# Rotary attention of one layer: the mix written to four column quadrants, the output product on the diagonal of the array, the normalisation on ScalarE, the output product ahead of the scores

## The chip, the cores and the metric

One core of a Trainium2 chip runs the whole program. The metric is the time of one execution on the device, in microseconds (us). Before the change the median of three runs is 3659.68 us.

## What is computed

The program is a twelve-stage model over x (128 sequences of 32 rows, 128 wide). The change touches the second stage only:

```python
x = x + _L0_attn_ref(_layernorm(x, axis=-1), L0_attn_Wq, L0_attn_Wk, L0_attn_Wv, L0_attn_Wo)

def _L0_attn_ref(x, Wq, Wk, Wv, Wo):      # HQ 16, HKV 4, HD 8, WINDOW 32
    xq, xk = _rope(x @ Wq), _rope(x @ Wk); xv = x @ Wv
    keys = jnp.repeat(xk, N_REP, axis=2)
    values = jnp.repeat(xv, N_REP, axis=2)
    scores = jnp.einsum('bqhd,bkhd->bhqk', xq, keys) / math.sqrt(HD)
    scores = jnp.where(mask[None, None], scores, -jnp.inf)
    attn = jax.nn.softmax(scores, axis=-1)
    ctx = jnp.einsum('bhqk,bkhd->bqhd', attn, values).reshape(b, s, HQ * HD)
    return ctx @ Wo
```

## The kernel before

`rotary_attention` (L573) works on 32 tiles; a tile is 4 sequences of 32 rows, so 128 partitions by 128 columns of x. Each engine runs one function `step(t, j, live)`, in which it handles several tiles that are at different ages: `live(lag)` says that tile t - lag exists. `pipelined` unrolls the first steps and the last eight, and puts those between into a hardware loop of four steps per turn. There are 32 tiles and four buffers (W = 4) of everything; `bank_a` and `bank_b` are the two PSUM banks of a buffer. Each engine does its instructions strictly as written, and waits on semaphores. So the written order inside `step` is what sets the order of the work:

- TensorE (L763): transpose of the normalised tile t (L166, after the addition to x of tile t - 4, whose bank it takes); transposes of the probabilities of t - 3 (`turn`, L746); projection of t to q and k (L729) and to v (L732); mix of t - 3 (L754); scores of t - 1 (L739); output product of t - 3 (L761).
- ScalarE (L655): copy of the transposed tile t (L173), of the transposed probabilities of t - 3 (L640), of v of tile t (L648), exponential of t - 2 (L644), copy of the mix of t - 3 (L652).
- VectorE (L698): addition to x of t - 4 (L186), rotary terms of t - 1 (L686, L690), band, maximum and subtraction of t - 2 (L677, L711, L713), moments of x of tile t + 2 (L119, L122), sum and reciprocal of t - 2 (L694, L696), normalisation of t + 1 (L160).
- GpSimd (L625): division of the probabilities of t - 3 (L622), inverse deviation of t + 1 (L135, L142), the two masked operands of t - 1 (L616, L618).

The mix of a tile is four matmuls, one for each sequence b. Each gives 32 rows (head group and head width) by 128 columns (head and query), and all four write partitions 0 to 31 of the bank, one beside the other. The copy reorders 32 x 512 values to `mixT`, and four matmuls, one for each head h of a group, accumulate the 128 rows of output from 32 rows each.

## Time and profile before

| | |
|---|---|
| median of 3 runs | 3659.68 us (3658.84 to 3660.41) |
| profiled execution, its own time | 3661.03 us |
| its span, first to last instruction | 3659.1 us |
| mean granted TensorE clock | 0.932 of 2.4 GHz |
| TensorE busy in the span | 3278.6 us (90%) |
| the stage of the change, first load to last addition | 91.6 to 306.0 us |

The profile gives for each engine when an instruction started, how long it took, and what ended the idle time before it. PE is TensorE's matmuls, PEld its weight loads (they overlap), DVE is VectorE, ACT ScalarE, POOL GpSimd, SP the queue that issues transfers. A matmul in 32-bit floats leaves two records, a transpose one. The stage is 6% of the program, and stages follow each other, so what the stage gains or loses the program does.

### The profile page before, as it was taken

Reading aid. Unit: us, or ns where it says so; the run is one execution under the profiler, and the core shown is the slowest. Engines: PE = TensorE matmul, PEld = TensorE weight load, DVE = VectorE, ACT = ScalarE, POOL = GpSimd, SP = SyncE. Lnnn points to the kernel's source line nnn. Section 1 sums busy time; section 2 is a strip of 40 time slices with the busy share of each in tenths; the row PEclk is TensorE's granted clock in tenths of the full one; section 3 lists DMA queues with packets and bytes.
Section 4 is the critical chain, followed back from the end, with each engine's and each line's share of the span. In section 5 each row is a group of like instructions: output and inputs, shape, how many; then the busy total and the mean of one; then the engine's idle time right before and its main releaser. Section 6 shows DMA issues by size and latency. Waiting matters only on the chain. (4 is left out here: it accounts for less than half of the span.)

```text
span 3659.1 us, 108450 instructions
## 1 busy us (share of the span) xinstructions
PE 3278.6 (90%) x40814; PEld 2737.0 (75%) x40816; DVE 2575.0 (70%) x7254; ACT 1817.8 (50%) x4530; POOL 1245.0 (34%) x1823
## 2 busy tenths in 40 slices
PE   6887899999989999897999999999999999874866
PEld 4776889898867777645789898899889899643345
DVE  6784999999968888757565655555655656468765
ACT  3331777777757777664433333333333333224463
POOL 3562888888843333312400000000000000155032
PEclk8997999999989999998799999999999999867687
DMA  4001000000012222200275555555555555254000
GB/s 117 5 0 38 1 0 0 0 0 0 0 48 78 79 78 77 72 1 7 60 139 132 131 132 132 122 139 127 133 131 127 132 130 131 69 108 74 0 3 26
DMA packets 375492, 254.10 MB, mean 69 GB/s; under 512 B 118676, under 2 KB 371560, under 8 KB 374536
## 3 DMA queue, kind: packets, MB, share of 16 engines
q1 hardware_dynamic: 370824, 245.44, 28.0%
q10 hardware_dynamic: 4352, 4.20, 0.5%
q8 instruction: 229, 3.75, 0.5%
q14 instruction: 87, 0.71, 0.1%
HBM read 233.53 MB, written 15.75 MB: 68 GB/s over the span
## 5 line engine op out<-in xcount | busy, mean ns | idle before, releaser
L1062 PE MATMUL psum<-L_ffn_share,L_ffn_prob 128*128 128x128 f32 x4096 | 491.1, 279 | 45.9 <-DVE L_ffn_prob L995 38.3
L1062 PEld LDWEIGHTS psum<-L_ffn_share,L_ffn_prob 128*128 128x128 f32 x4096 | 473.5, 193 | 59.5 <-DVE L_ffn_prob L995 46.2
L878 POOL TENSOR_TENSOR L_ffn_sums<-L_ffn_sims 128x1024 f32<-128x1024 f32 x256 | 485.3, 1912 | 85.8 <-DVE L_ffn_prob L995 85.8
L2463 PE MATMUL psum<-L_xattn_ctxT,L_xattn_q_ctx 128*128 128x257 f32 x2048 | 510.6, 390 | 0.0
L2494 PEld LDWEIGHTS psum<-L_xattn_probT,L_xattn_ctx 32*128 32x128 f32 x16384 | 469.1, 187 | 44.6 <-issue 42.0
L2494 PE MATMUL psum<-L_xattn_probT,L_xattn_ctx 32*128 32x128 f32 x16384 | 493.4, 273 | 2.1 <-DVE L_xattn_probT L2377 2.1
L2315 ACT ACTIVATE L_xattn_prob<-psum,L_xattn_nmax 128x258 f32<-128x258 f32 x512 | 239.2, 472 | 480.1 <-DVE L_xattn_nmax L2363 463.5
L2286 POOL TENSOR_TENSOR L_xattn_z_var<-L_xattn_z_mv,L_xattn_z_eps 128x1 f32<-128x1 f32 x32 | 6.1, 192 | 1248.6 <-DVE L_xattn_z_mv L2389 1219.3
L2463 PEld LDWEIGHTS psum<-L_xattn_ctxT,L_xattn_q_ctx 128*128 128x128 f32 x2048 | 368.5, 191 | 62.2 <-issue 5.9
L920 ACT ACTIVATE psum<-L_ffn_sums,L_ffn_bias 128x512 f32<-128x512 f32 x512 | 339.2, 686 | 89.1 <-DVE L_ffn_prob L995 85.1
L995 DVE SCALAR_TENSOR_TENSOR L_ffn_prob<-L_ffn_sums,L_ffn_best,psum 128x512 f32<-128x512 f32 x512 | 358.1, 741 | 6.9 <-ACT psum L920 3.8
L1352 ACT ACTIVATE L_xattn_prob<-psum,L_xattn_nmax 128x289 f32<-128x289 f32 x512 | 250.0, 501 | 109.0 <-DVE L_xattn_nmax L1383 109.0
L2368 DVE RECIPROCAL L_xattn_total<-L_xattn_total 128x2 f32<-128x2 f32 x256 | 41.4, 162 | 245.7 <-ACT L_xattn_prob L2315 235.3
L1383 DVE TENSOR_REDUCE L_xattn_nmax<-psum 128x1 f32<-128x289 f32 x512 | 199.1, 451 | 14.2 <-PE psum L1421 7.9
L2309 ACT ACTIVATE L_xattn_q_heads<-psum 128x256 f32<-128x256 f32 x128 | 49.2, 384 | 320.3 <-PE psum L2435 320.3
L2377 DVE STREAM_TRANSPOSE L_xattn_probT<-L_xattn_prob 128x512 f32<-128x512 f32 x256 | 182.2, 712 | 19.4
L2363 DVE TENSOR_REDUCE L_xattn_nmax<-psum 128x2 f32<-128x516 f32 x256 | 178.2, 696 | 19.1 <-issue 0.4
L2371 DVE TENSOR_SCALAR L_xattn_prob<-L_xattn_prob,L_xattn_total 128x256 f32<-128x256 f32 x512 | 158.4, 351 | 21.6 <-issue 2.1
L2353 DVE COPY L_xattn_q_ctx<-psum 128x512 f32<-128x512 f32 x256 | 159.8, 664 | 17.1 <-PE psum L2447 17.1
L1421 PE MATMUL psum<-L_xattn_k_all,L_xattn_q_bd 32*128 32x289 f32 x1024 | 153.0, 460 | 13.7 <-DMA L_xattn_k_all<-ctx_T_dram 4.0
L2447 PE MATMUL psum<-L_xattn_q_heads,L_xattn_wk_cross 64*128 64x128 f32 x2048 | 154.3, 291 | 7.7 <-issue 5.2
L1437 PEld LDWEIGHTS psum<-const,L_xattn_prob 128*128 128x128 f32 x1024 | 111.3, 142 | 51.1 <-issue 49.9
(459 smaller groups left out, 6651.0 us busy)
## 6 DMA issues: line engine op xcount, KB each, us to landing
L_xattn_ctx<-ctx_dram SPq DMA_DIRECT2D x512, 256.0 KB, 3.9
L_xattn_ctxT<-ctx_T_dram SPq DMA_DIRECT2D x128, 257.0 KB, 3.3
L_xattn_k_all<-ctx_T_dram SPq DMA_DIRECT2D x128, 128.5 KB, 2.1
L_xattn_v_all<-ctx_dram SPq DMA_DIRECT2D x128, 128.0 KB, 2.2
L_attn_qkv_scratch<-L_attn_qkv SPq DMA_DIRECT2D x24, 256.0 KB, 2.8
L_attn_rows<-L_attn_qkv_scratch SPq DMA_DIRECT2D x24, 256.0 KB, 5.3
start_raw<-ctx_dram ACTq DMA_DIRECT2D x16, 256.0 KB, 11.9
L_xattn_v_rows<-L_xattn_v SPq DMA_DIRECT2D x8, 256.0 KB, 2.3
```

The lines of the kernel that those rows point to most:

```text
L878: nc.gpsimd.tensor_tensor(sums[:, h % RING, :, :], sx, sy, ALU.add).then_inc(summed, 1)
L920: nc.scalar.activation(raw_prob(k), half(sums[:, h % RING, :, :].rearrange("p i j -> p (i j)"), k), ACT.Exp, bias=bias[:, s, h:h + 1]).the ...
L995: nc.vector.scalar_tensor_tensor(half(prob[:, h % RING, :], k), half(sums[:, h % RING, :, :].rearrange("p i j -> p (i j)"), k), best[:, s, ...
L1062: last = nc.tensor.matmul(pair(2 * s)[:, c * P:(c + 1) * P], prob[:, h % RING, c * P:(c + 1) * P], share[:, h % RING, :], start=(h == 0 an ...
L1352: ins = nc.scalar.activation(prob[:, b % 2, g, :], scores(g), ACT.Exp, bias=nmax[:, b % 2, g:g + 1], accum_out=total[:, b % 2, g:g + 1])
L1383: nc.vector.tensor_reduce(nmax[:, b % 2, g:g + 1], scores(g), X, ALU.max, negate=True).then_inc(maxed, 1)
L2315: ins = nc.scalar.activation(prob[:, s, g, :], scores(s)[:, g, :], ACT.Exp, bias=nmax[:, s, g:g + 1], accum_out=total[:, s, g:g + 1])
L2353: nc.vector.tensor_copy(q_ctx[:, t % 2, c, :, 4 * j:4 * j + 4, :], core.psum[:, 2:4, :].rearrange("p e (a w) -> p (e a) w", a=2)[:, :, c * ...
L2363: nc.vector.tensor_reduce(nmax[:, s, :], scores(s), X, ALU.max, negate=True).then_inc(maxed, 1)
L2377: nc.vector.transpose(probT[:, b % 2, :, 2 * s:2 * s + 2, :].rearrange("p k g n -> p g k n"), prob[:, s, :, 0:2 * P].rearrange("p g (k m) ...
L2463: last = nc.tensor.matmul(scores(s)[:, g, 0:CTX], q_ctx[:, p, c, b, h:h + 4, :].rearrange("p h n -> p (h n)"), ctxT[:, b, c, :], start=(c ...
L2494: last = nc.tensor.matmul(mix_bank(r)[:, c * P:(c + 1) * P], ctx[rows, b, k, c * P:(c + 1) * P], probT[rows, b % 2, k, :, :].rearrange("p ...
```

## The change

- `mix`: the matmul of sequence b writes partitions 32b to 32b + 31, columns 0 to 127, so the four use four different column groups of the array. `mix_copy` copies 128 x 128 values without reordering in place of 32 x 512.
- `out`: sixteen matmuls in place of four. The one of head h and sequence b has rows 32b to 32b + 31 of `mixT` and `w_o`, and writes the same partitions of the bank: the diagonal 32 x 32 tiles of the array, b innermost. `w_o` holds the same weights four times, loaded with four transfers in place of one.
- `out` of tile t - 3 stands ahead of `score` of tile t - 1 on TensorE.
- The addition to x is that of tile t - 3, in the same step, after the moments and ahead of the sums on VectorE (before: of tile t - 4, first thing of the next step).
- The normalisation of t + 1 goes from VectorE (L160) to ScalarE, as an activation between the copy of v and the exponential. GpSimd gets one more small instruction a tile for its bias.
- TensorE's steps are all unrolled, without the hardware loop.

```diff
--- before.py
+++ after.py
@@ -582,7 +582,7 @@
         w_qk = sb("w_qk", [D, 4, D])
 
         w_v = sb("w_v", [D, G, G * 8])
-        w_o = sb("w_o", [G * 8, G, D])
+        w_o = sb("w_o", [P, G, D])
         qk = sb("qk", [P, W, 2, P])
         prod = sb("prod", [P, W, 2, P])
         q4 = sb("q4", [P, W, BT, G, SEQ])
@@ -591,20 +591,21 @@
         prob = sb("prob", [P, W, HEADS, SEQ])
         top = sb("top", [P, W, HEADS])
         total = sb("total", [P, W, HEADS])
+        shifted_mean = sb("shifted_mean", [P, W])
         probT = sb("probT", [P, W, BT, P])
-        mixT = sb("mixT", [G * 8, W, G, P])
+        mixT = sb("mixT", [P, W, G, SEQ])
         bank_a = lambda s: core.psum[:, 2 * s, :]
         bank_b = lambda s: core.psum[:, 2 * s + 1, :]
         front = Front(core, st, name, W, bank_a)
         (w_in, zeroed, projected, v_done, roped, masked, scored, shifted, exped, summed, normal, turned, probT_done,
-         mixed, mixT_done, out_done, added) = (core.sem(f"{name}_{n}") for n in (
+         mixed, mixT_done, out_done, added, centred) = (core.sem(f"{name}_{n}") for n in (
              "w_in", "zeroed", "projected", "v_done", "roped", "masked", "scored", "shifted", "exped", "summed",
-             "normal", "turned", "probT_done", "mixed", "mixT_done", "out_done", "added"))
+             "normal", "turned", "probT_done", "mixed", "mixT_done", "out_done", "added", "centred"))
         block = st.enter_context(nc.Block())
 
         @block.sync
         def _(sp):
-            load(sp, [(w_qk[:, :, :], dram[f"{name}_Wqk"]), (w_o[:, :, :], dram[f"{name}_Wo"])], w_in)
+            load(sp, [(w_qk[:, :, :], dram[f"{name}_Wqk"]), *((w_o[32 * b:32 * b + 32, :, :], dram[f"{name}_Wo"]) for b in range(BT))], w_in)
             sp.wait_ge(zeroed, 1)
             load(sp, [(w_v[:, g, 8 * g:8 * g + 8], dram[f"{name}_Wv"][:, 8 * g:8 * g + 8]) for g in range(G)], w_in)
 
@@ -617,6 +618,12 @@
                 a, m = spread(qk[:, s, 1, :].rearrange("p (b w) -> p b w", b=BT), core.c("group"), SEQ)
                 nc.gpsimd.tensor_tensor(kbd[:, s, :, :, :], a, m, ALU.mult).then_inc(masked, 1)
 
+            def normal_factors(t, s):
+                front.pool_rstd(pool, t - s, only=s)
+                pool.drain()
+                nc.gpsimd.tensor_scalar(shifted_mean[:, s:s + 1], front.mv[:, s, 0:1], front.rstd[:, s, :], -1.0, ALU.mult,
+                                        ALU.mult).then_inc(centred, 1)
+
             def normalise(t, s):
                 pool.wait_ge(summed, t + 1)
                 nc.gpsimd.tensor_tensor(prob[:, s, :, :], prob[:, s, :, :], per_row(total[:, s, :]),
@@ -626,7 +633,7 @@
                 if live(3):
                     normalise(t - 3, (j - 3) % W)
                 if live(-1):
-                    front.pool_rstd(pool, t + 1 - (j + 1) % W, only=(j + 1) % W)
+                    normal_factors(t + 1, (j + 1) % W)
                 if live(1):
                     mask(t - 1, (j - 1) % W)
 
@@ -639,6 +646,11 @@
                 act.wait_ge(turned, t + 1)
                 nc.scalar.copy(probT[:, s, :, :], bank_a(s).rearrange("p (b w) -> p b w", b=BT)).then_inc(probT_done, 1)
 
+            def normalise(t, s):
+                act.wait_ge(centred, t + 1)
+                nc.scalar.activation(front.xn[:, s, :], core.x[:, ds(t, 1), :].rearrange("p a d -> p (a d)"), ACT.Identity,
+                                     bias=shifted_mean[:, s:s + 1], scale=front.rstd[:, s, :]).then_inc(front.normed, 1)
+
             def exp(t, s):
                 act.wait_ge(shifted, t + 1)
                 nc.scalar.activation(prob[:, s, :, :], prob[:, s, :, :], ACT.Exp).then_inc(exped, 1)
@@ -649,8 +661,7 @@
 
             def mix_copy(t, s):
                 act.wait_ge(mixed, t + 1)
-                nc.scalar.copy(mixT[:, s, :, :].rearrange("p h (b q) -> p b h q", b=BT),
-                               bank_b(s)[0:G * 8, :].rearrange("p (b h q) -> p b h q", b=BT, h=G)).then_inc(mixT_done, 1)
+                nc.scalar.copy(mixT[:, s, :, :], bank_b(s)[:, 0:P].rearrange("p (h q) -> p h q", h=G)).then_inc(mixT_done, 1)
 
             def step(t, j, live):
                 if live(0):
@@ -659,6 +670,8 @@
                     turn_copy(t - 3, (j - 3) % W)
                 if live(0):
                     v_copy(t, j)
+                if live(-1):
+                    normalise(t + 1, (j + 1) % W)
                 if live(2):
                     exp(t - 2, (j - 2) % W)
                 if live(3):
@@ -696,10 +709,7 @@
                 nc.vector.reciprocal(total[:, s, :], total[:, s, :]).then_inc(summed, 1)
 
             def step(t, j, live):
-                o, q = (j - 1) % W, (j - 2) % W
-                if live(4):
-                    dve.wait_ge(out_done, t - 3)
-                    add_to_x(core, t - 4, bank_a(j)[:, 0:D]).then_inc(added, 1)
+                o, q, m = (j - 1) % W, (j - 2) % W, (j - 3) % W
                 if live(1):
                     turn_pairs(t - 1, o)
                     dve.drain()
@@ -713,10 +723,11 @@
                     nc.vector.tensor_tensor(prob[:, q, :, :], raw, per_row(top[:, q, :]), ALU.subtract).then_inc(shifted, 1)
                 if live(-2):
                     front.dve_moments(dve, t + 2 - (j + 2) % W, only=(j + 2) % W)
+                if live(3):
+                    dve.wait_ge(out_done, t - 2)
+                    add_to_x(core, t - 3, bank_a(m)[:, 0:D]).then_inc(added, 1)
                 if live(2):
                     sums(t - 2, q)
-                if live(-1):
-                    front.dve_normalise(dve, t + 1 - (j + 1) % W, only=(j + 1) % W)
 
             front.dve_moments(dve, 0, only=0)
             pipelined(dve, W, -1, 4, step)
@@ -751,14 +762,17 @@
                 pe.wait_ge(v_done, t + 1)
                 pe.wait_ge(probT_done, t + 1)
                 for b in range(BT):
-                    last = nc.tensor.matmul(bank_b(s)[0:G * 8, b * P:(b + 1) * P], vbd[:, s, b, :], probT[:, s, b, :],
+                    last = nc.tensor.matmul(bank_b(s)[32 * b:32 * b + 32, 0:P], vbd[:, s, b, :], probT[:, s, b, :],
                                             start=True, stop=True)
                 last.then_inc(mixed, 1)
 
             def out(t, s):
                 pe.wait_ge(mixT_done, t + 1)
                 for h in range(G):
-                    last = nc.tensor.matmul(bank_a(s)[:, 0:D], mixT[:, s, h, :], w_o[:, h, :], start=(h == 0), stop=(h == G - 1))
+                    for b in range(BT):
+                        own = slice(32 * b, 32 * b + 32)
+                        last = nc.tensor.matmul(bank_a(s)[own, 0:D], mixT[own, s, h, :], w_o[own, h, :], start=(h == 0),
+                                                stop=(h == G - 1))
                 last.then_inc(out_done, 1)
 
             def step(t, j, live):
@@ -772,13 +786,14 @@
                     project(t, j)
                 if live(3):
                     mix(t - 3, (j - 3) % W)
+                if live(3):
+                    out(t - 3, (j - 3) % W)
                 if live(1):
                     score(t - 1, (j - 1) % W)
-                if live(3):
-                    out(t - 3, (j - 3) % W)
-
-            pe.wait_ge(w_in, 16 * (2 + G))
-            pipelined(pe, W, -1, 4, step)
+
+            pe.wait_ge(w_in, 16 * (1 + BT + G))
+            for t in range(TILES + 4):
+                step(t, t % W, lambda lag: 0 <= t - lag < TILES)
 
 
 def product_key_experts(core, name):
```

Below, rows of the order in which the engines are given their work, first VectorE, from the band addition of one step to the addition to x. Before:

```order
L677 TENSOR_TENSOR psum<-psum,const 128x512
L711 TENSOR_REDUCE L_attn_top<-psum 128x16
L713 TENSOR_TENSOR L_attn_prob<-psum,L_attn_top 128x512
L119 ISA
L119 BN_STATS L_attn_front_stats_sb<-x_sb 128x6
L122 BN_AGGR L_attn_front_mv_sb<-L_attn_front_stats_sb 128x2
L694 TENSOR_REDUCE L_attn_total<-L_attn_prob 128x16
L696 RECIPROCAL L_attn_total<-L_attn_total 128x16
L160 TENSOR_SCALAR L_attn_front_xn_sb<-x_sb,L_attn_front_mv_sb,L_attn_front_rstd_sb 128x128
L186 ISA
L186 TENSOR_TENSOR x_sb<-x_sb,psum 128x128
```

VectorE, the same stretch of the changed kernel (its line numbers differ: L690, L721, L723 are the band, maximum and subtraction, L707 and L709 the sum and the reciprocal, L699 the first rotary product):

```order
L690 TENSOR_TENSOR psum<-psum,const 128x512
L721 TENSOR_REDUCE L_attn_top<-psum 128x16
L723 TENSOR_TENSOR L_attn_prob<-psum,L_attn_top 128x512
L119 ISA
L119 BN_STATS L_attn_front_stats_sb<-x_sb 128x6
L122 BN_AGGR L_attn_front_mv_sb<-L_attn_front_stats_sb 128x2
L186 ISA
L186 TENSOR_TENSOR x_sb<-x_sb,psum 128x128
L707 TENSOR_REDUCE L_attn_total<-L_attn_prob 128x16
L709 RECIPROCAL L_attn_total<-L_attn_total 128x16
L699 TENSOR_TENSOR psum<-psum,const 128x2x128
```

The addition L186 has moved from behind the sum and the reciprocal to ahead of them, and L160 is gone. ScalarE, one step of before:

```order
L173 COPY L_attn_front_xnT_sb<-psum 128x128
L640 COPY L_attn_probT<-psum 128x512
L648 COPY L_attn_vbd<-psum 128x128
L644 ACTIVATE L_attn_prob<-L_attn_prob 128x512
L652 COPY L_attn_mixT<-psum 32x4x4x32
```

and of the change (L656 is the exponential, L664 the copy of the mix):

```order
L173 COPY L_attn_front_xnT_sb<-psum 128x128
L647 COPY L_attn_probT<-psum 128x512
L660 COPY L_attn_vbd<-psum 128x128
L650 REGISTER_ALU
L651 ISA
L651 ACTIVATE L_attn_front_xn_sb<-x_sb,L_attn_shifted_mean,L_attn_front_rstd_sb 128x128
L656 ACTIVATE L_attn_prob<-L_attn_prob 128x512
L664 COPY L_attn_mixT<-psum 128x128
```

The normalisation L651 stands between the copy of v and the exponential, and the copy of the mix is still behind the exponential. TensorE, one step of before:

```order
L166 MATMUL psum<-const,L_attn_front_xn_sb 128x128
L746 MATMUL psum<-const,L_attn_prob 128x128 x4
L729 MATMUL psum<-L_attn_front_xnT_sb,L_attn_w_qk 128x128 x4
L732 MATMUL psum<-L_attn_w_v,L_attn_front_xnT_sb 32x32 x16
L754 MATMUL psum<-L_attn_probT,L_attn_vbd 32x128 x4
L739 MATMUL psum<-L_attn_kbd,L_attn_q 128x128 x4
L761 MATMUL psum<-L_attn_w_o,L_attn_mixT 128x128 x4
```

and of the change (L757 turns the probabilities, L740 and L743 project, L765 mixes, L774 is the output product, L750 the scores):

```order
L166 MATMUL psum<-const,L_attn_front_xn_sb 128x128
L757 MATMUL psum<-const,L_attn_prob 128x128 x4
L740 MATMUL psum<-L_attn_front_xnT_sb,L_attn_w_qk 128x128 x4
L743 MATMUL psum<-L_attn_w_v,L_attn_front_xnT_sb 32x32 x16
L765 MATMUL psum<-L_attn_probT,L_attn_vbd 32x128 x4
L774 MATMUL psum<-L_attn_w_o,L_attn_mixT 32x128 x16
L750 MATMUL psum<-L_attn_kbd,L_attn_q 128x128 x4
```

The output product has gone ahead of the scores and is sixteen matmuls of 32 output rows.

## Rows read from the trace of the kernel before

**Rows 1.** By stretch: length, PE, PEld, DVE, ACT, POOL busy (records), clock, DMA share, GB/s:
```profile
150.00:200.00 50.00, 44.30 (x563) 36.76 (x560) 40.52 (x100) 18.69 (x42) 30.67 (x41) 1.00 0.00 0
```

**Rows 2.** Timeline of one step: start, us, engine, line, operation [idle before <-releaser]
```profile
217.25 0.63 ACT L644 ACTIVATE L_attn_prob<-L_attn_prob 128x512 f32<-128x512 f32 x1 [0.63 <-DVE L_attn_prob L713]
...
217.79 0.56 ACT L652 COPY L_attn_mixT<-psum 32x512 f32<-32x512 f32 x1
...
218.40 1.15 PE L761 MATMUL psum<-L_attn_w_o,L_attn_mixT 32*128 32x128 f32 x8
...
219.70 0.29 DVE L186 TENSOR_TENSOR x_sb<-x_sb,psum 128x128 f32 x1 [0.53 <-PE psum L761]
...
220.80 1.16 PE L729 MATMUL psum<-L_attn_front_xnT_sb,L_attn_w_qk 128*128 128x128 f32 x8
...
221.89 0.46 PE L732 MATMUL psum<-L_attn_w_v,L_attn_front_xnT_sb 128*32 128x32 f32 x32
...
222.16 1.04 PE L754 MATMUL psum<-L_attn_probT,L_attn_vbd 128*32 128x128 f32 x8
...
222.43 0.27 ACT L648 COPY L_attn_vbd<-psum 128x128 f32<-128x128 f32 x1 [0.92 <-PE psum L732]
222.60 0.69 DVE L713 TENSOR_TENSOR L_attn_prob<-psum,L_attn_top 128x512 f32<-128x512 f32 x1
223.33 0.63 ACT L644 ACTIVATE L_attn_prob<-L_attn_prob 128x512 f32<-128x512 f32 x1 [0.64 <-DVE L_attn_prob L713]
...
223.99 0.69 DVE L694 TENSOR_REDUCE L_attn_total<-L_attn_prob 128x16 f32<-128x512 f32 x1
...
224.75 0.25 DVE L696 RECIPROCAL L_attn_total<-L_attn_total 128x16 f32<-128x16 f32 x1
```

**Rows 3.** Timeline, an early step where TensorE waited for the divided probabilities:
```profile
108.48 0.25 DVE L696 RECIPROCAL L_attn_total<-L_attn_total 128x16 f32<-128x16 f32 x1
...
108.82 1.05 POOL L622 TENSOR_TENSOR L_attn_prob<-L_attn_prob,L_attn_total 128x512 f32<-128x512 f32 x1 [2.77 <-DVE L_attn_total L696]
...
109.92 0.42 PEld L746 LDWEIGHTS psum<-const,L_attn_prob 128*128 128x128 f32 x4 [0.82 <-POOL L_attn_prob L622]
...
110.31 0.97 PEld L729 LDWEIGHTS psum<-L_attn_front_xnT_sb,L_attn_w_qk 128*128 128x128 f32 x8
```

**Rows 4.** Timeline, ScalarE: normalising activations of another stage, a copy ahead of the exponential:
```profile
75.60 1.65 ACT L494 ACTIVATE L_xattn_front_xn_sb<-x_sb,L_xattn_shifted,L_xattn_front_rstd_sb 128x128 f32<-128x128 f32 x4 [2.37 <-POOL L_xattn_shifted L476]
...
106.89 0.27 ACT L648 COPY L_attn_vbd<-psum 128x128 f32<-128x128 f32 x1 [1.68 <-PE psum L732]
107.06 0.64 ACT L644 ACTIVATE L_attn_prob<-L_attn_prob 128x512 f32<-128x512 f32 x1
```

**Rows 5.** Timeline, TensorE in two later attention stages: quarter-array matmuls that rotate over groups:
```profile
1303.38 0.65 PE L1470 MATMUL psum<-L_xattn_probT,L_xattn_v_all 128*32 128x128 f32 x16
1303.84 0.40 PE L1473 MATMUL psum<-L_xattn_endT,L_xattn_v_end 128*32 128x128 f32 x8
...
2399.73 1.83 PE L2494 MATMUL psum<-L_xattn_probT,L_xattn_ctx 32*128 32x128 f32 x57
```

**Rows 6.** Timeline, start of the stage, and the bias instruction in the next stage:
```profile
92.47 1.84 SPq L180 DMA_DIRECT2D L_attn_w_v<-L_attn_Wv_dram  x4
...
95.69 0.48 PE L166 MATMUL psum<-const,L_attn_front_xn_sb 128*128 128x128 f32 x1 [5.12 <-DMA L_attn_w_v<-L_attn_Wv_dram]
...
357.51 0.27 POOL L855 TENSOR_SCALAR L_ffn_shifted_mean<-L_ffn_front_mv_sb,L_ffn_front_rstd_sb 128x1 f32<-128x1 f32 x1 [0.20 <-issue]
```

**Rows 7.** Timeline: additions to x on either side of a fall of the clock:
```profile
121.25 0.29 DVE L186 TENSOR_TENSOR x_sb<-x_sb,psum 128x128 f32 x1 [0.53 <-PE psum L761]
...
128.45 0.29 DVE L186 TENSOR_TENSOR x_sb<-x_sb,psum 128x128 f32 x1 [1.19 <-PE psum L761]
```

**Rows 8.** Busy time by stretch: around the second fall, and in a later attention stage:
```profile
242.00:248.00 6.00, 5.43 (x62) 4.80 (x61) 4.91 (x13) 1.58 (x5) 3.81 (x5) 0.72 0.00 0
...
3300.00:3340.00 40.00, 29.33 (x659) 25.35 (x659) 38.90 (x75) 20.16 (x45) 33.97 (x46) 1.00 0.79 110
```

## The prediction

> **What bounds the kernel now.** I read three views: the busy time by stretch, to see whether an engine is full in this stage; the timeline of one step, for what each engine waits on; and the timeline of the stage's start. In the first [rows 1] TensorE is busy 44.3 of 50 us, VectorE 40.5, ScalarE only 18.7. No engine is full, so a ring of waits must set the pace. The reader should look at the exponential in the second view [rows 2]: it starts at 217.25 and again at 223.33, so a step is 6.08 us. The ring is closed like this. The subtraction starts at 222.60 and the exponential 0.73 later. The copy of the mix stands behind it on ScalarE and starts 0.54 after it (217.25 to 217.79). The output product starts 0.61 later (218.40), the addition to x 1.30 after that (219.70), and the next subtraction on VectorE 2.90 after the addition (222.60). 0.73 + 0.54 + 0.61 + 1.30 + 2.90 = 6.08, the whole step. VectorE idles 0.53 us in it, right before the addition, for the output product. The sum and the reciprocal are not in this ring: VectorE does them while ScalarE and TensorE finish the mix and the output.
>
> **The mix in quadrants** takes TensorE work away. Now it is 8 records in 1.04 us on one column group [rows 2]; 8 records that rotate over four groups took 0.40 [rows 5]. That is 0.6 us of TensorE a step, but the mix is not in the ring (its copy waits for the exponential), so I count 0. Its copy shrinks from 32 x 512 (0.56) to 128 x 128, which is the size of the copy of v (0.27) [rows 2]: minus 0.29 in the ring.
>
> **The output product** becomes 32 records of a quarter tile with 128 columns each. No row shows the diagonal. The nearest rows are quarter-array matmuls with 128 columns that rotate over groups: 16 records from 1303.38 to 1303.84, 29 ns each, and 57 in 1.83 us, 32 ns each [rows 5]. 32 of them are 0.92 to 1.03, and the last one's own tail adds about 0.2 (0.65 against 0.46 in the first row). I take 1.15, as now, because the rows with 128 columns are nearer than any other. The bounds: 0.46, which the 32 records with 32 columns took [rows 2], and 4.2, if they ran one after another like the mix of before (1.04 for 8). The rows for four row groups have one bank for each group; here all four write one bank, though different partitions. The Trainium skill (TensorEngine Tiling (Array Packing), Restrictions and Gotchas) says that different row tiles cannot access the same PSUM bank at once. By it the sum would be that of the serial rival below; by the rotating rows it is the 1.15. No trace here has row groups that share a bank, so neither is shown.
>
> **The addition ahead of the sums** is the costly edit. The output product of t - 3 still waits for the copy of the mix, which waits behind the exponential of t - 2. VectorE, which reaches the addition right after the moments, must now wait through exponential, copy and product, and only then does it sum and invert. Both were off the ring and come onto it: 0.76 for the sum (223.99 to 224.75) and 0.17 until the next instruction starts (the reciprocal is 0.25 long; the copy of v, 0.27 long, frees its engine after 0.17 [rows 4]). Ring: 6.08 - 0.29 + 0.76 + 0.17 = 6.72. Taking 0.26 us of normalisation off VectorE is worth nothing, since it stood in the time in which VectorE would have waited.
>
> **The normalisation on ScalarE** closes a longer ring. It stands behind the copy of v of tile t, and the exponential behind it. From the start of one reciprocal: 0.34 until GpSimd divides, 1.10 until TensorE turns, 0.39 until it projects [rows 3]; 1.09 until v, 0.54 until v is copied [rows 2]; 0.17 until the next ScalarE instruction, 0.41 for the normalisation (four in 1.65) [rows 4]; 0.54 for the exponential until the copy of the mix, 0.27 + 0.05 until the output product, 1.15 + 0.15 until the addition [rows 2]; 0.21 until the sum (an addition of 0.29, freeing the engine early as above), 0.76 until the next reciprocal. The sum is **7.17 us**, longer than 6.72, so this ring sets the step: plus 1.09. The exponential will start some 0.5 us after its subtraction has ended instead of 0.04.
>
> **The rest.** Scores behind the output product: with four matmuls of the projection's size (1.09 [rows 2]) they end about 4.90 + 1.15 + 1.09 = 7.1 into the step. The band addition wants them in the next step behind its rotary terms, so after 7.17 + 0.17. The cover is over 0.2 us, so 0; were it gone, the wait would come onto VectorE's part of the ring. GpSimd's new instruction: 0.20 idle and 0.27 [rows 6]; the masked operands come up to 0.5 later and still ahead of the scores' turn behind the product, so 0. Unrolled TensorE steps: the unrolled first steps of before ran without a gap of their own [rows 3], so 0. The three extra transfers of `w_o` stand ahead of those of `w_v` on SP's queue, four of which took 1.84 us, and TensorE's first transpose waits for the last of them [rows 6]: 3 x 0.46 = +1.4, once.
>
> **The clock.** Between the additions at 121.25 and 128.45 [rows 7] the step took 7.20, 1.12 more than normal; a stretch around the second such step shows a granted clock of 0.72, part of it at 1.2 GHz, although TensorE was 90% busy [rows 8]. There are two in the full steps of before. The change spreads less TensorE work over a longer step, with a gap before the output product and one before the turn, so I expect more of them. A later attention stage held 2.4 GHz through at 29.3 of 40 us busy [rows 8], which bounds the price from below at 0. From above I take 20 falls at 1.12, +22. I take four, +4, nearer the lower end because that stage's row is the one with comparable gaps.
>
> **The sum.** 28 steps have all ages in flight: 28 x 1.09 = 30.5. Three more drain without a projection and follow the 6.72 ring: 3 x 0.64 = 1.9. Transfers 1.4, clock 4. Together +38. The profiled execution took 3661.03 us, so 3699; the median of the runs shown is 1.35 below it. Forecast against the median: **3698 us**, 1.0% slower. About 0.2%, 7 us, is what a measurement of this kernel can tell from no change.
>
> **Rivals.**
> - *The clock falls often.* Every second or third step has a stretch at 1.2 GHz. For: it fell even at 90% busy [rows 8]. Against: the later stage at 73%. +34 + 22 = 3715 to 3722.
> - *The diagonal runs serially* (shared bank, as above): product 3.5 to 4.2 instead of 1.15, plus 2.4 to 3.0 on 31 steps, about 3780.
> - *Only the VectorE ring binds*, because the normalisation finds ScalarE free earlier than I think: 6.72 a step, 31 x 0.64 = 20, plus 1.4 and a little clock: about 3682.
> - *The other side: faster.* If the output product were ready when VectorE reaches the addition, VectorE's own work would be the bound: 6.08 less the 0.53 of waiting and less the 0.26 of L160, 5.3 us. 28 x -0.78 = -22, so 3639. It decides only if the product no longer waits for an exponential on ScalarE. The order on ScalarE (mix copy last) speaks plainly against it.
> - *No change*: a product near its lower bound 0.46 makes the rings 6.48 and 6.03; the first still costs 12 us. So this needs that and an error in the ring as well.
>
> **How the numbers follow.** Chances: the forecast 0.60, frequent clock falls 0.20, the VectorE ring alone 0.08, serial diagonal 0.06, faster 0.03, no change 0.03. The range takes in the first three, with a shorter product than 1.15 on the low side: 3680 to 3724, which leaves out 0.12 and a little. Faster 0.03, same 0.03, slower 0.94.
>
> **What would show it.** Reciprocals 7.2 us apart; VectorE idle some 2 us before L186, put down to TensorE; on ScalarE copy of v, normalisation and exponential back to back, the exponential 0.5 after the subtraction's end; the product 1.15 long; the mix 0.4; TensorE's first transpose near 97.1; a stage of some 252 us and TensorE busy near 65% of it. I am wrong if the steps are 6.1 or shorter, if the product is much longer than 1.2, or if the gain or loss lies in another stage.

## The result, and the profile of the changed kernel

| | before | changed |
|---|---|---|
| median of the runs | 3659.26 us (4 runs, 3658.09 to 3660.41) | 3687.06 us (4 runs, 3685.05 to 3687.74) |
| ratio | | 1.0075, 95% interval 1.0058 to 1.0093 |
| profiled execution, its own time | 3661.03 us | 3686.7 us |
| its span | 3659.1 us | 3684.9 us |
| the stage, first load to last addition | 91.62 to 306.02 us | 87.87 to 333.31 us |

The change makes the kernel 0.75% slower, 28 us. The forecast was 3698 us with a range of 3680 to 3724, so the direction, the range and the mechanism held, and the size was 11 us too high. One execution of the kernel before (7460 us, granted clock 0.42) and one of `scores_first` (5261 us, 0.56) fell in a slow state and are left out below, where `scores_first` therefore has a median of 3719.4 us and not the 3721.7 that one expectation quotes.

Busy time by stretch of the changed kernel (length, PE, PEld, DVE, ACT, POOL busy with records, clock, DMA share, GB/s), for [rows 1]:

```profile
150.00:200.00 50.00, 31.93 (x658) 25.99 (x656) 33.36 (x78) 15.32 (x42) 28.08 (x42) 1.00 0.01 2
200.00:250.00 50.00, 31.44 (x652) 25.61 (x651) 33.54 (x80) 15.59 (x43) 28.35 (x43) 1.00 0.01 2
```

TensorE's busy time fell from 44.3 to 31.9 of 50 us and VectorE's from 40.5 to 33.4, while the clock stayed at 2.4 GHz. Both engines wait longer in a step, and both have a little less to do in it (the mix takes 0.45 us instead of 1.04, and VectorE no longer normalises). Where they wait is seen in one step of its timeline, for [rows 2 to 4]:

```profile
200.00 0.25 DVE L709 RECIPROCAL L_attn_total<-L_attn_total 128x16 f32<-128x16 f32 x1
...
200.34 1.05 POOL L629 TENSOR_TENSOR L_attn_prob<-L_attn_prob,L_attn_total 128x512 f32<-128x512 f32 x1 [2.71 <-DVE L_attn_total L709]
...
201.44 0.66 PE L757 MATMUL psum<-const,L_attn_prob 128*128 128x128 f32 x4 [1.38 <-POOL L_attn_prob L629]
...
202.92 0.46 PE L743 MATMUL psum<-L_attn_w_v,L_attn_front_xnT_sb 128*32 128x32 f32 x32
203.08 0.69 DVE L723 TENSOR_TENSOR L_attn_prob<-psum,L_attn_top 128x512 f32<-128x512 f32 x1
203.19 0.45 PE L765 MATMUL psum<-L_attn_probT,L_attn_vbd 128*32 128x128 f32 x8
203.45 0.27 ACT L660 COPY L_attn_vbd<-psum 128x128 f32<-128x128 f32 x1 [0.73 <-PE psum L743]
203.62 0.49 ACT L651 ACTIVATE L_attn_front_xn_sb<-x_sb,L_attn_shifted_mean,L_attn_front_rstd_sb 128x128 f32 x1
...
204.03 0.61 ACT L656 ACTIVATE L_attn_prob<-L_attn_prob 128x512 f32<-128x512 f32 x1
...
204.54 0.24 ACT L664 COPY L_attn_mixT<-psum 128x128 f32<-128x128 f32 x1
204.84 1.07 PE L774 MATMUL psum<-L_attn_w_o,L_attn_mixT 32*32 32x128 f32 x32 [1.20 <-ACT L_attn_mixT L664]
205.85 1.16 PE L750 MATMUL psum<-L_attn_kbd,L_attn_q 128*128 128x128 f32 x8
206.10 0.29 DVE L186 TENSOR_TENSOR x_sb<-x_sb,psum 128x128 f32 x1 [1.59 <-PE psum L774]
206.31 0.68 DVE L707 TENSOR_REDUCE L_attn_total<-L_attn_prob 128x16 f32<-128x512 f32 x1
...
207.06 0.25 DVE L709 RECIPROCAL L_attn_total<-L_attn_total 128x16 f32<-128x16 f32 x1
```

The lines are the forecast's longer ring, in its order. From reciprocal to reciprocal the starts lie 0.34, 1.10, 1.48 (turn to v), 0.53, 0.17, 0.41, 0.51, 0.30, 1.26, 0.21 and 0.75 us apart: 7.06 us a step, where 7.17 was forecast and 6.08 was the time before. The subtraction L723 ends at 203.77 and its exponential starts at 204.03, because v's copy and the normalisation stand ahead of it. VectorE then idles 1.59 us for the product (0.53 before), and the sum and the reciprocal come only behind that. This step is one of every fourth, in which the first rotary product starts 0.38 us behind the reciprocal; in the three others it starts 0.17 behind, the exponential starts 0.49 after the end of the subtraction, and the wait for the product is 1.82 us. The step is 7.06 us in all four, so VectorE's delay stays hidden behind the longer ring. Why it comes once in four steps is not traced.

The start of the stage, for [rows 6]:

```profile
88.25 1.81 SPq L180 DMA_DIRECT2D L_attn_w_o<-L_attn_Wo_dram  x4
90.10 1.85 SPq L180 DMA_DIRECT2D L_attn_w_v<-L_attn_Wv_dram  x4
93.30 0.47 PE L166 MATMUL psum<-const,L_attn_front_xn_sb 128*128 128x128 f32 x1 [6.49 <-DMA L_attn_w_v<-L_attn_Wv_dram]
```

TensorE's first transpose is 5.43 us behind the stage's first load at 87.87; before it was 95.69 - 91.62 = 4.07. That is +1.36 for three more transfers.

**Where the 28 us are.** In the profiled executions the stage is 245.4 us long instead of 214.4, so +31.0. From the first load to the first addition it takes 26.4 us instead of 23.5 (+2.9, of which 1.36 are transfers and the rest longer first steps). In those the clock was low just when the first tile's product ran, which took 1.93 us instead of 1.07:

```profile
110.00:117.00 7.00, 5.74 (x85) 4.21 (x85) 3.72 (x11) 1.60 (x5) 3.17 (x5) 0.51 0.01 2
```

```profile
112.30 1.93 PE L774 MATMUL psum<-L_attn_w_o,L_attn_mixT 32*32 32x128 f32 x32 [1.02 <-ACT L_attn_mixT L664]
```

The next 28 additions lie 196.8 us apart in all instead of 172.0 (+24.8). The last three take 22.0 instead of 18.6 (+3.3); the granted clock is 0.50 in 18.4 us of this part, and in 10 us of it before. Outside the stage the changed kernel's execution was 5.2 us shorter, 3.75 of them ahead of it, in code that nobody touched. I do not count that part as an effect of the change: among the kernels of the experiments the stage begins anywhere from 88 to 92 us, and no edit goes with it (88.3 in `unrolled_alone`, which has the smallest edit of all, 91.4 in `quadrants_unrolled`).

### The profile page after: what moved, and what is told of

Its sections match the earlier page's. It is cut to its first block and busy times, and to the rows that moved or that the text cites. A ratio compares the mean times of both kernels' runs of the same rounds, so it can differ in the third digit from the quotient of the medians.

```text
span 3684.9 us, 110052 instructions
## 1 busy us (share of the span) xinstructions
PE 3238.7 (88%) x41582; PEld 2698.9 (73%) x41584; DVE 2566.7 (70%) x7222; ACT 1816.5 (49%) x4562; POOL 1253.3 (34%) x1855
## 5 line engine op out<-in xcount | busy, mean ns | idle before, releaser
L935 ACT ACTIVATE psum<-L_ffn_sums,L_ffn_bias 128x512 f32<-128x512 f32 x512 | 339.3, 686 | 92.3 <-DVE L_ffn_prob L1010 88.3
L2352 ACT COPY L_xattn_mixed_ctx<-psum 128x1024 f32<-128x1024 f32 x128 | 129.6, 1013 | 39.4 <-PE psum L2509 39.4
```

The lines of the kernel that those rows point to most:

```text
L935: nc.scalar.activation(raw_prob(k), half(sums[:, h % RING, :, :].rearrange("p i j -> p (i j)"), k), ACT.Exp, bias=bias[:, s, h:h + 1]).the ...
```

## The experiments

The theory: the step is set by the ring that the timeline shows, and it is dear because the late addition puts the sum and the reciprocal behind a product that itself waits behind an exponential. The rivals: the normalisation on ScalarE is the dear part; the diagonal product or the unrolled program is; or the clock is. Ratios are to the kernel before, run on the same chip in the same session (medians 3658.7, 3659.7 and 3662.6 us in the three sessions; times from different sessions can differ by as much).

**`sums_first`**: the changed kernel, only VectorE's order changed.

```diff
                     front.dve_moments(dve, t + 2 - (j + 2) % W, only=(j + 2) % W)
+                if live(2):
+                    sums(t - 2, q)
                 if live(3):
                     dve.wait_ge(out_done, t - 2)
                     add_to_x(core, t - 3, bank_a(m)[:, 0:D]).then_inc(added, 1)
-                if live(2):
-                    sums(t - 2, q)
```

> The changed kernel with one edit: on VectorE the sum and the reciprocal stand ahead of the addition to x instead of behind it. Ring theory (the step is 7.06 us because VectorE waits for the output product before it sums): sum and reciprocal leave the ring, and the longest one left is subtraction, exponential, copy of the mix, output product, addition, rotary terms: 0.73 + about 0.4 for the normalisation ahead of the exponential at times + 0.54 + 0.30 + 1.22 + 2.90, so 5.7 to 5.8 us a step, and about 3648 us, 39 under the change. Rival theory (the loss is the normalisation on ScalarE or the unrolled TensorE code, not the place of the addition): no move, 3687 us, steps of 7.0.

Measured: 3648.3 us, ratio 0.9968 (0.9958 to 0.9977). Its timeline:

```profile
209.03 0.63 ACT L656 ACTIVATE L_attn_prob<-L_attn_prob 128x512 f32<-128x512 f32 x1
...
209.69 0.69 DVE L707 TENSOR_REDUCE L_attn_total<-L_attn_prob 128x16 f32<-128x512 f32 x1
...
209.86 1.08 PE L774 MATMUL psum<-L_attn_w_o,L_attn_mixT 32*32 32x128 f32 x32 [1.28 <-ACT L_attn_mixT L664]
210.45 0.25 DVE L709 RECIPROCAL L_attn_total<-L_attn_total 128x16 f32<-128x16 f32 x1
...
211.12 0.29 DVE L186 TENSOR_TENSOR x_sb<-x_sb,psum 128x128 f32 x1 [0.42 <-PE psum L774]
```

The sum now runs while TensorE multiplies, and only 0.42 us of waiting is left. Seventeen steps take 98.0 us, 5.76 each. One exchange of two calls is worth 38.7 us: the place of the sums accounts for more than the whole loss, and with it gone the rest of the change gains 10 us by the medians, 12 by the ratio.

**`xn_vector`**: the changed kernel with the normalisation back on VectorE.

```diff
# ScalarE
-                if live(-1):
-                    normalise(t + 1, (j + 1) % W)
# VectorE, behind the sums
+                if live(-1):
+                    front.dve_normalise(dve, t + 1 - (j + 1) % W, only=(j + 1) % W)
```

> The changed kernel with the normalisation back on VectorE, as its last instruction in a step; the bias instruction on GpSimd is gone. Two-ring theory: the ring over GpSimd, TensorE and ScalarE loses 0.41 and the one over VectorE, now with 0.17 of normalisation in it, sets the step at 6.8 us; about 8 us under the change, 3679. Rival (the normalisation on ScalarE is hidden or VectorE's relief is worth its 0.17): 0 to 5 us slower than the change.

Measured: 3680.9 us, ratio 1.0057 (1.0039 to 1.0075); fifteen steps in 103.4 us, 6.90 each. Its exponential follows the subtraction at once, so this is the VectorE ring:

```profile
187.59 0.69 DVE L721 TENSOR_TENSOR L_attn_prob<-psum,L_attn_top 128x512 f32<-128x512 f32 x1
```

```profile
188.31 0.63 ACT L656 ACTIVATE L_attn_prob<-L_attn_prob 128x512 f32<-128x512 f32 x1
```

The forecast gave 6.72 for that ring, and 0.17 for the normalisation back on the engine makes 6.89. The agreement is partly luck: the undisturbed steps are 6.81, and every fourth is 7.12 to 7.14, by the delay of the first rotary product that the longer ring hides in the changed kernel. The normalisation on ScalarE costs 6 us of the 28, not the bulk. The intervals of the two ratios overlap; the traces show it, with the stage 239.1 us long instead of 245.4.

**`quadrants_unrolled`** and **`unrolled_alone`**: the kernel before with the new layout (mix in quadrants, diagonal product, four loads) and the unrolled program, and with the unrolled program alone.

```diff
-            pipelined(pe, W, -1, 4, step)
+            for t in range(TILES + 4):
+                step(t, t % W, lambda lag: 0 <= t - lag < TILES)
```

> The kernel of before with the layout alone: mix in four column quadrants, its copy 128 x 128, output product on the diagonal, four loads of the output weights, TensorE's steps unrolled. Addition, scores and normalisation stay as they were. Ring theory: the copy of the mix is 0.29 shorter in the ring of 6.08, the scores ahead of the product then delay it a little: 5.85 us a step, minus 7, plus 1.4 for the transfers, so 3654 us, 5 under before. Rival (the mix was never on the path, so nothing moves): 3660.

> The kernel of before with TensorE's steps of this stage unrolled, nothing else. Ring theory: the hardware loop costs nothing on the ring, steps stay 6.08, 3659 us within 0.1%. Rival (fetching straight-line code costs, or the loop's register instructions did): 2 us or more either way.

Measured: 3654.1 us, ratio 0.9983 (0.9973 to 0.9992), and 3659.9 us, ratio 1.0001 (0.9992 to 1.0011). The hardware loop costs nothing that shows. The layout gives 5 us. The time is the expected one, partly by luck: the steps are 5.97 us (sixteen in 95.5 us) and not the expected 5.85, which is 3 us over 28 steps, and the rest is that the two falls of the clock of before are absent, 2.3 us. Its mix copy takes 0.25 us in place of 0.56, but most of that is lost. In its timeline of TensorE and ScalarE the copy is done at 205.54, and TensorE is at the scores until it takes up the product at 205.84:

```profile
204.75 1.16 PE L738 MATMUL psum<-L_attn_kbd,L_attn_q 128*128 128x128 f32 x8 [0.79 <-POOL L_attn_kbd L618]
205.84 1.08 PE L762 MATMUL psum<-L_attn_w_o,L_attn_mixT 32*32 32x128 f32 x32
```

```profile
205.29 0.25 ACT L652 COPY L_attn_mixT<-psum 128x128 f32<-128x128 f32 x1
```

So neither the layout nor the unrolling is behind the loss. The new order on TensorE, scores behind the product, takes this wait away in the changed kernel.

**`scores_first`**: the changed kernel with the scores ahead of the product again.

```diff
-                if live(3):
-                    out(t - 3, (j - 3) % W)
                 if live(1):
                     score(t - 1, (j - 1) % W)
+                if live(3):
+                    out(t - 3, (j - 3) % W)
```

> The changed kernel with the scores of t - 1 ahead of the output product of t - 3 on TensorE, as before the change. Ring theory: the product now waits for the masked operands and then for 0.97 us of scores, so it starts 0.8 to 0.9 us later in every step: 7.9 us a step, about 24 us over the change, 3711. Rival (the order of the two does not matter, since TensorE is idle for over 2 us a step): no move, 3687.

Measured: 3719.4 us, the median of three, ratio 1.0172 (1.0150 to 1.0194). TensorE's order is the part that helps most. Without it the product stands behind scores that wait for GpSimd's masked operands, and the loss is 61 us:

```profile
204.55 1.16 PE L750 MATMUL psum<-L_attn_kbd,L_attn_q 128*128 128x128 f32 x8 [1.09 <-POOL L_attn_kbd L619]
205.64 1.08 PE L774 MATMUL psum<-L_attn_w_o,L_attn_mixT 32*32 32x128 f32 x32
```

The result is 8 us above what was expected; `scores_first_filled` below asks why.

**`late_add_alone`**: the kernel before with the late addition and nothing else.

```diff
-                if live(4):
-                    dve.wait_ge(out_done, t - 3)
-                    add_to_x(core, t - 4, bank_a(j)[:, 0:D]).then_inc(added, 1)
...
+                if live(3):
+                    dve.wait_ge(out_done, t - 2)
+                    add_to_x(core, t - 3, bank_a(m)[:, 0:D]).then_inc(added, 1)
                 if live(2):
                     sums(t - 2, q)
```

> The kernel of before with one edit: the addition to x is that of t - 3, ahead of the sums, as in the change; mix, product, TensorE's order, the normalisation and the hardware loop are those of before. Ring theory: sum, reciprocal and normalisation (0.76 + 0.17 + 0.17) come onto the ring, and the scores ahead of the product delay it: 7.2 to 7.6 us a step, 3700 to 3706 us, so more than the whole loss of the change, and the other parts win some 15 us of it back. Rival (the addition is a small part of the loss): under 3670.

Measured: 3771.9 us, ratio 1.0308 (1.0289 to 1.0326), 66 us above the expectation's upper end. Its stretches and TensorE's timeline:

```profile
150.00:200.00 50.00, 39.46 (x382) 32.66 (x381) 24.77 (x61) 11.30 (x27) 19.04 (x26) 0.70 0.00 0
200.00:250.00 50.00, 39.58 (x347) 32.60 (x346) 24.75 (x62) 11.15 (x27) 18.82 (x25) 0.67 0.00 0
```

```profile
236.99 1.92 PE L729 MATMUL psum<-L_attn_front_xnT_sb,L_attn_w_qk 128*128 128x128 f32 x8
238.84 0.66 PE L732 MATMUL psum<-L_attn_w_v,L_attn_front_xnT_sb 128*32 128x32 f32 x32
239.29 1.90 PE L754 MATMUL psum<-L_attn_probT,L_attn_vbd 128*32 128x128 f32 x8
```

The projection takes 1.92 us instead of 1.16, the mix 1.90 instead of 1.04 [rows 2]: these run at 1.2 GHz. All of TensorE's work but the first transpose lies in this variant's ring (reciprocal, turn, projection, mix, scores, product, addition, sum), so what the low clock adds to it the step gets in full. The steps are 8.7 to 10.2 us long, 9.75 in the mean of 28.

**`late_out_first`**: the same with the product ahead of the scores.

> The kernel of before with the late addition (as in late_add_alone) and with the output product ahead of the scores, in the old layout and with the hardware loop. By the rings at full clock: 7.2 us a step, 3696 us. Theory A (the order, scores directly ahead of the product, made TensorE's clock fall in late_add_alone): few falls, 3696 to 3702. Theory B (the old layout, mix and product each on a quarter of the array one after another, made it fall): falls in most steps as in late_add_alone, 3730 or more.

Measured: 3708.1 us, ratio 1.0129 (1.0112 to 1.0146). It lies between the two theories. Its shortest full steps are 7.16 to 7.17 us, as worked out, and others 8.7; the granted clock is 0.90 and 0.97 in the same two stretches. So the order of the product gives back 64 us here, where the undisturbed steps differ by 0.48 us (7.65 in `late_add_filled`, below), 13 us over 28 steps. Most of it is the clock. The product still waits for its copy on TensorE, 0.7 to 1.0 us in most steps and 1.30 once:

```profile
212.29 1.15 PE L761 MATMUL psum<-L_attn_w_o,L_attn_mixT 32*128 32x128 f32 x8 [0.99 <-ACT L_attn_mixT L652]
```

**`late_add_filled`** and **`scores_first_filled`**: four added matmuls a step whose result nobody reads, where TensorE waited.

```diff
+            def fill(s):
+                for b in range(BT):
+                    nc.tensor.matmul(bank_b(s)[:, b * P:(b + 1) * P], core.c("ident"), core.c("ident"), start=True, stop=True)
...
                     if live(4):
+                        fill(j)
                         pe.wait_ge(added, t - 3)
```

> The kernel before with the late addition alone, and in each full step four matmuls of the identity with itself on TensorE, ahead of the first transpose, where it waited 1.6 us for the normalised tile. They take 1.16 us at full clock, so they fit into that wait, and nothing reads what they write. Theory A (of the 112 us that the late addition alone cost, most was the low clock, 0.67 to 0.70, and the ring of waits is only about 7.6 us at full clock): with the gap filled the granted clock stays near 1.00 and the time falls by 60 us to 3700 to 3710, although TensorE has more to do. Theory B (the ring itself is that long, and the low clock only goes with it): the time stays at 3770 or rises by what the added matmuls take, to 3780 and more.

> The changed kernel with the scores ahead of the output product, which took 3721.7 us with a granted clock of 0.93 in the full steps, and the same four added matmuls ahead of the first transpose of each full step. There TensorE waited 0.5 us, and 1.7 us more behind that transpose for the divided probabilities, so 1.16 us delay the transpose by some 0.6 and the turn by nothing. Theory A (about 11 us of that result were falls of the clock): clock near 1.00 in the full steps, 3708 to 3714. Theory B (the ring is 0.4 us a step longer than worked out, whatever the clock): 3720 or more.

Measured: 3726.2 us, ratio 1.0168 (1.0151 to 1.0185), and 3718.2 us, ratio 1.0145 (1.0128 to 1.0162). The same stretches of the first:

```profile
150.00:200.00 50.00, 42.99 (x462) 36.72 (x462) 30.04 (x74) 13.34 (x31) 22.63 (x31) 0.90 0.00 0
200.00:250.00 50.00, 42.66 (x468) 36.43 (x469) 30.45 (x74) 13.45 (x32) 23.82 (x34) 0.92 0.00 0
```

and of `scores_first`, then of its filled form:

```profile
150.00:200.00 50.00, 31.14 (x559) 24.64 (x559) 29.15 (x70) 13.40 (x37) 24.08 (x36) 0.93 0.01 1
```

```profile
150.00:200.00 50.00, 35.22 (x647) 29.24 (x646) 28.66 (x68) 13.12 (x36) 24.02 (x36) 1.00 0.01 2
```

The late addition alone becomes 46 us faster (51 by the ratios) by being given 1.16 us more work a step. Its clock rises from 0.68 to 0.91, and its undisturbed steps are 7.65 us, so the ring was sized right: 28 x (7.65 - 6.08) = 44 us, some 3704. It did not reach that, since about every second or third step still falls to 1.2 GHz, so theory A holds in kind and not in full. The second pair is less clear. Filled, its steps lie 8.02 us apart at a clock of 1.00, and the 28 take 223.2 us instead of 230.0. So the falls cost 7 us in the traced execution of `scores_first`: 0.15 us a step where they are light (seventeen steps in 139.0 us, 8.18 each), and two early steps of 9.8 and 9.1. The ring was short by about 3 us besides (8.03 where 7.9 was worked out, 0.12 on 28 steps). But the filled form loses 1.7 us again ahead of its first addition and 0.8 behind the 28, so the stage gains 4.4 us only. Against the kernel before of its own session `scores_first` was 61 us slower and the filled form 56. As a time, 3718 lies between the two theories, nearer B; but its session was 4 us slower for the kernel before as well, and with that taken off it is at the upper end of theory A. Both causes are there, and the clock is the larger one in the full steps.

**`copy_first`**: the changed kernel with the copy of the mix ahead of the exponential, the normalisation behind it, and the sums as in `sums_first`.

```diff
                     v_copy(t, j)
-                if live(-1):
-                    normalise(t + 1, (j + 1) % W)
-                if live(2):
-                    exp(t - 2, (j - 2) % W)
                 if live(3):
                     mix_copy(t - 3, (j - 3) % W)
+                if live(2):
+                    exp(t - 2, (j - 2) % W)
+                if live(-1):
+                    normalise(t + 1, (j + 1) % W)
```

> The changed kernel with the sums ahead of the addition (as in sums_first) and on ScalarE the copy of the mix ahead of the exponential and the normalisation behind it. Ring theory: nothing waits for the exponential but the sum, no ring is longer than VectorE's own work, 5.3 us a step, so 28 x 0.45 = 13 us under sums_first: 3635 us. Rival (in sums_first another wait, over TensorE, already sets the step): 3645 or more.

Measured: 3633.2 us, ratio 0.9927 (0.9911 to 0.9944), faster than both kernels. Its timeline:

```profile
206.38 0.27 ACT L664 COPY L_attn_mixT<-psum 128x128 f32<-128x128 f32 x1
206.56 0.63 ACT L656 ACTIVATE L_attn_prob<-L_attn_prob 128x512 f32<-128x512 f32 x1
206.70 1.08 PE L774 MATMUL psum<-L_attn_w_o,L_attn_mixT 32*32 32x128 f32 x32 [0.35 <-ACT L_attn_mixT L664]
...
207.22 0.69 DVE L707 TENSOR_REDUCE L_attn_total<-L_attn_prob 128x16 f32<-128x512 f32 x1
...
207.98 0.25 DVE L709 RECIPROCAL L_attn_total<-L_attn_total 128x16 f32<-128x16 f32 x1
208.15 0.27 DVE L186 TENSOR_TENSOR x_sb<-x_sb,psum 128x128 f32 x1
```

The product is done before VectorE comes to the addition, which has no wait any more. Seventeen steps take 89.9 us, 5.29 each, which is VectorE's own work: the forecast's rival on the faster side gave 5.3. ScalarE's edit moves two things, the copy of the mix ahead of the exponential and the normalisation behind it; neither was run without the other.

**`copy_first_late`**: the same with the addition back ahead of the sums.

> The fastest variant so far (3633.2: mix copy ahead of the exponential, normalisation behind it, sums ahead of the addition) with the addition put back ahead of the sums, where the change has it. Theory A (the late addition costs little by itself once the product does not wait for the exponential, but the output product, the addition and the sum now stand in the ring through GpSimd and TensorE, 0.33 + 1.10 + 0.39 + 1.10 + 0.53 + 0.22 + 0.32 + 1.23 + 0.21 + 0.76 = 6.2 us against 5.3): 0.9 us on 28 steps, 3656 to 3662, the time of the kernel before. Theory B (only the exponential ahead of the product made the late addition dear, and VectorE's own work of 5.3 us sets the step either way): 3633 to 3640.

Measured: 3661.2 us, ratio 0.9994 (0.9985 to 1.0004); sixteen steps in 99.3 us, 6.21 each, VectorE idle again:

```profile
205.69 0.29 DVE L186 TENSOR_TENSOR x_sb<-x_sb,psum 128x128 f32 x1 [0.98 <-PE psum L774]
206.65 0.25 DVE L709 RECIPROCAL L_attn_total<-L_attn_total 128x16 f32<-128x16 f32 x1
```

So two orders were at fault, and each makes the other dearer. By the ratios the late addition costs 25 us even when no exponential stands ahead of the product, and 39 when one does; ScalarE's order costs 15 us with the sums first and 30 with the addition first.

**`copy_first_wo_last`**: `copy_first` with the loads of `w_o` behind those of `w_v`, on a semaphore of their own.

```diff
-            load(sp, [(w_qk[:, :, :], dram[f"{name}_Wqk"]), *((w_o[32 * b:32 * b + 32, :, :], dram[f"{name}_Wo"]) for b in range(BT))], w_in)
+            load(sp, [(w_qk[:, :, :], dram[f"{name}_Wqk"])], w_in)
...
+            load(sp, [(w_o[32 * b:32 * b + 32, :, :], dram[f"{name}_Wo"]) for b in range(BT)], wo_in)
```

> The fastest variant so far (3633.2), with the four loads of the output weights put behind those of the v weights and with a semaphore of their own, for which TensorE waits at the first output product. Theory A (the four transfers ahead of the v weights delay the first transpose of the stage by 1.36 us, and the loads of all other weights by 0.46 more each): 1.4 to 1.9 us less, 3631 to 3632, which is within what can be told apart but should show in the trace as a first transpose 1.5 us or more earlier after the stage's start. Theory B (the start is hidden by something else): no shift of the first addition to x against the start of the stage.

Measured: 3631.6 us, ratio 0.9908 (0.9891 to 0.9924). The first transpose is at 96.23, 3.85 us behind the stage's first load at 92.38; in `copy_first` it was 93.88 - 88.27 = 5.61. The traces show the 1.76 us, and 1.0 of it at the first addition (23.60 us behind the first load instead of 24.64). The medians, 1.7 us apart, are of different sessions and can't show it. It is the fastest version found, 28 us below the kernel before by the medians of the earlier sessions and 31 by its own.

## Why the prediction was right, and where its sizes were off

- **The addition ahead of the sums, the costly edit.** Right. Sum and reciprocal stand behind the product in the timeline, and taking them from there gives back 38.7 us.
- **The normalisation closes the longer ring.** Right. The waits are those of the sum: in three of four steps the exponential starts 0.49 us after the subtraction's end, where 0.5 was forecast, and VectorE idles 1.82 us for the product, where some 2 was. Taking the normalisation out of it (`xn_vector`) left the VectorE ring, 6.90 us; that 6.72 + 0.17 gives the same number is partly luck, as shown there.
- **The ring, 7.17.** It is 7.06. The product's term (start to addition) was 1.26 instead of 1.30, the exponential's 0.51 instead of 0.54, the copy's 0.30 instead of 0.32, and v and the sum 0.01 each less. Over 28 steps that is 3 us.
- **The output product, 1.15.** It took 1.07. The four diagonal tiles wrote different partitions of one bank, and their 32 records took 1.07 us, 33 ns each, near the 29 to 32 ns of tiles that rotate over groups [rows 5]. So the serial rival, 3.5 to 4.2 us, is out. The Trainium skill (TensorEngine Tiling (Array Packing), Restrictions and Gotchas) says that different row tiles cannot access the same PSUM bank simultaneously. The trace does not bear that out for tiles that write different partitions of the bank; row tiles that write the same partitions were not tried.
- **The clock, +4.** This is the mis-sized term. I expected more falls in a stage that is less busy. There were none in the full steps, and the two falls of before [rows 7, 8] went as well, 2.3 us. So in the full steps the term was -2 and not +4, 6 us of the 11. It was reasoned from gaps, and the gaps did not decide. At both ends the clock cost something that the forecast had in no term: 0.86 us at the first tile's product, and a part of the last three steps that I did not separate.
- **Transfers, +1.4.** Right in size: 1.36. The longer first steps, 1.5 us more (0.86 of it the slow product), were not in the sum, and the drain was +3.3, not +1.9.
- **The sum.** Measured in the stage: 2.9 + 24.8 + 3.3 = 31.0 where 38 were forecast. The profiled executions differ by only 25.7; the other 5 us lie outside the stage. So part of the 11 us is no error of the ring or the clock but the scatter of code that nobody touched.
- **The faster rival** was placed correctly: it "decides only if the product no longer waits for an exponential". `copy_first` fulfils that and reaches it, but `copy_first_late` shows that this condition alone isn't enough; the sums must be ahead of the addition too.
- **TensorE's new order** was costed as harmless. It is more than that: without it the changed kernel would take some 33 us more (`scores_first`; 32 by the medians, 34 by the length of the stage), and the late addition on the kernel before 64.

## What to carry to other kernels

When work is moved to an earlier place on an in-order engine, look at what it waits for and then at what stands behind it: here a wait of 1.6 to 1.8 us was put ahead of two instructions that the next tile's whole ring needs. The instruction whose input comes last belongs last, on VectorE (the addition) as on ScalarE (the exponential ahead of a short copy that TensorE awaits). When several edits are timed together, time each against the whole: three of these gain or cost little, one exchange of two calls costs 39 us, and undoing it and turning round ScalarE's order made a gain of 26 us out of a loss of 28.

## What the runs showed of the hardware that I had not expected

- TensorE's clock did not follow its busy share. It stayed at 2.4 GHz with TensorE 63% busy in the changed kernel, fell twice with 89% before, and was at 0.67 to 0.70 with 79% in `late_add_alone`. Added matmuls in a wait brought that to 0.91, and in `scores_first` from 0.93 to 1.00. What separates these patterns isn't settled. The longest single wait doesn't: 1.39 us in the full steps of the changed kernel without a fall, 1.30 in `late_out_first` with one every few steps, and 0.64 before with two. Every variant with the old layout fell in its full steps (0.96 in `unrolled_alone`), and of those with the new one only `scores_first` did. The new layout alone held the clock, with TensorE 78% busy, as the first row shows, of `quadrants_unrolled`; the second is the same stretch of `unrolled_alone`, with the old layout:

```profile
112.00:285.00 173.00, 135.04 (x2698) 108.85 (x2699) 141.66 (x343) 54.82 (x144) 109.21 (x144) 1.00 0.01 2
```

```profile
112.00:285.00 173.00, 154.85 (x1928) 130.15 (x1927) 136.08 (x329) 61.41 (x140) 105.02 (x138) 0.96 0.01 1
```

  That points to the layout, but a second comparison of that kind wasn't made, and each kernel was profiled once.
- A low clock is dearest where TensorE's work lies in the ring: there the step of 7.65 us becomes 9.75 in the mean, and a term of 44 us becomes 113. Whether the longer step then keeps the clock low isn't shown.
- Four 32 x 32 tiles on the diagonal of the array ran side by side although they wrote into one PSUM bank: 32 records with 128 columns in 1.07 us, 33 ns each.
